# Selective scan of a 12-block decoder: two states in one scan instruction, the residual added by TensorE, the normalisation done by ScalarE

## The reference, cut to what matters

```
gate = sigmoid(x @ W_gate.T + b_gate)
x_proj, delta_proj = split(x @ W_in.T + b_in)
delta = relu(delta_proj)
A = -exp(A_log);  c0 = C_mat[0]
for each time step t:                  # h: batch x 512 channels x 16 states
    h = h * exp(A * delta_t) + (x_t * delta_t) * B_mat
    y_t = h @ c0
block = gate * (y + x_proj * D_vec) @ W_out.T + b_out
x = layernorm(x + block)
```

## Time and profile before

| | |
|---|---|
| median of 3 runs | 3064.9 us (3063.79 to 3069.06) |
| profiled execution | 3043.24 us, of which the span is 3041.4 us |
| granted TensorE clock, mean of the span | 0.972 |
| PE busy | 2806.5 us, 92% |
| DVE busy | 1905.0 us, 63% |
| ACT busy | 1218.6 us, 40% |
| POOL busy | 324.8 us, 11% |
| the scan block | from 2365 to 2705 us of the span |

### The profile page before, as it was taken

How to read it: one execution, slowest core, us unless ns; L and a number is a source line. 1 busy time by engine, 2 the same in 40 slices (tenths; PEclk the granted TensorE clock), 3 DMA queues, 4 the chain that set the end, 5 groups by cost and what they waited for, 6 DMA issues and landing times. The chain is left out here.

```text
span 3041.4 us, 52348 instructions
## 1 busy us (share of the span) xinstructions
PE 2806.5 (92%) x20888; PEld 1815.5 (60%) x20888; DVE 1905.0 (63%) x3430; ACT 1218.6 (40%) x2591; POOL 324.8 (11%) x459
## 2 busy tenths in 40 slices
PE   6999899999998979899999989899898899989898
PEld 3565456666666858566666667656565333346576
DVE  4675367777764347477777753345557999966522
ACT  1333254445542335355544431133242866633111
POOL 1111100000002700000000000000111000001232
PEclk9999999999999979899999999999999999999899
DMA  3001000000012331100000000100000000000241
GB/s 117 20 14 69 23 33 5 5 5 5 5 67 78 92 127 37 42 5 5 8 6 5 36 18 1 33 17 21 19 21 32 18 1 1 1 18 18 101 168 66
DMA packets 43246, 103.58 MB, mean 34 GB/s; under 512 B 4929, under 2 KB 32687, under 8 KB 39425
## 3 DMA queue, kind: packets, MB, share of 16 engines
q1 hardware_dynamic: 37217, 86.66, 8.1%
q0 software_dynamic: 5792, 13.59, 1.5%
HBM read 66.74 MB, written 19.07 MB: 28 GB/s over the span
## 5 line engine op out<-in xcount | busy, mean ns | idle before, releaser
L2350 ACT ACTIVATE prob<-R,neg_max 128x333 f32<-128x333 f32 x512 | 268.7, 538 | 184.0 <-DVE neg_max L2417 183.8
L3898 DVE TENSOR_TENSOR_SCAN arena<-arena,u 128x512 f32<-128x512 f32 x256 | 289.5, 1200 | 0.3 <-issue 0.2
L2238 PEld LDWEIGHTS T<-const,prob 128*128 128x128 f32 (+1 forms) x1536 | 183.6, 143 | 82.4 <-DVE prob L2430 37.0
L2430 DVE TENSOR_TENSOR prob<-prob,rec 128x666 f32<-128x666 f32 x256 | 218.4, 853 | 19.8 <-issue 0.9
L2417 DVE TENSOR_REDUCE neg_max<-R 128x2 f32<-128x666 f32 x256 | 205.8, 845 | 34.9 <-PE R L2227 34.8
L2238 PE MATMUL T<-const,prob 128*128 128x128 f32 (+1 forms) x1536 | 211.0, 274 | 13.0 <-DVE prob L2430 10.7
L2357 ACT ACTIVATE prob_t<-T 128x384 f32<-128x384 f32 x256 | 125.8, 491 | 228.4 <-PE T L2238 222.3
L3829 ACT ACTIVATE arena<-delta,neg_a 128x510 f32<-128x510 f32 x256 | 174.5, 714 | 40.2 <-DVE arena L3898 39.1
L2423 DVE COPY prob_t<-T 128x384 f32<-128x384 f32 x256 | 142.3, 556 | 39.5 <-PE T L2238 13.0
L2157 PE MATMUL O<-keys_in,arena 128*128 128x333 f32 x512 | 164.8, 444 | 0.0
L3732 PE MATMUL R<-arena,diag 64*64 64x512 f32 x1024 | 136.0, 620 | 27.4 <-DVE arena L3898 27.3
(11 more groups left out here) (590 smaller groups left out, 5341.6 us busy)
## 6 DMA issues: line engine op xcount, KB each, us to landing
w<-w_dram SPq DMA_DIRECT2D x16, 1024.0 KB, 6.9
arena<-pack_dram SPq DMA_DIRECT2D x2, 4100.0 KB, 14.6
q_pad<-q_pad SPq DMA_DIRECT2D x24, 224.0 KB, 2.7
arena<-pack_dram SPq DMA_DIRECT2D x4, 1284.0 KB, 6.6
arena<-pack_dram SPq DMA_DIRECT2D x1, 4896.0 KB, 15.3
slots_in<-x_nat SPq DMA_DIRECT2D x2, 2048.0 KB, 8.7
arena<-planes SPq DMA_DIRECT2D x8, 512.0 KB, 8.5
arena<-k_nat SPq DMA_DIRECT2D x16, 224.0 KB, 2.7
```

The source lines that it names most:

```text
L2238: last = nc.tensor.transpose(S.T[0:n, i, kc * P:(kc + 1) * P], prob[:, g % 2, i, first:first + n], S.ident)
L2350: last = nc.scalar.activation(prob[:, g % 2, i, :], S.R[:, g % 2, i * BANK:i * BANK + XK], ACT.Exp, bias=neg_max[:, g % 2, i:i + 1], accum ...
L2430: nc.vector.tensor_tensor(prob[:, g % 2, :, :], prob[:, g % 2, :, :], rec[:, g % 2, :].unsqueeze(2).to_broadcast([P, 2, XK]), ALU.mult)\
L3898: nc.vector.tensor_tensor_scan(state[:, q % HELD, :], decay[:, q % DEEP, :], u[:, i % 2, :], 0.0, ALU.mult, ALU.add)\
```

## The change

Six edits, all in `selective_scan`:

1. A scan instruction covers two states: 1024 elements instead of 512, from two adjacent ring slots. There are 128 instead of 256. The rings keep their sizes (6 and 10 slots). The scan waits for both decays. Since `u` must then stand twice in a row, ScalarE copies it (`doubled`), once a unit.
2. The first two decays and the first copy of `u` are issued ahead of the wait for `setup_bc`.
3. The residual is added by TensorE: a matmul of the identity with `x_nat` behind each bias matmul, 16 matmuls in all (32 as recorded).
4. VectorE's `residual` and `normalised` go. What stays is `spread`: statistics read straight from PSUM. It stands behind the scans of states 10 and 11, and of 12 and 13, of a leaving unit (before: behind states 12 and 15, and the two normalisations behind state 15 and behind state 2 of the next unit). The statistics have a slot for each of two batches.
5. GpSimd makes a shift, -mean * rstd, besides rstd: four instructions with two drains instead of two with one. ScalarE normalises from PSUM with scale and bias (`normalised`), at `n == 13` and `n == 15` of a leaving unit.
6. ScalarE's copy of the second batch to `x_t` moves from `n == 12` to `n == 8` of the following unit. TensorE's transposes stay where they were.

The core of the diff (left out: names of marks and buffers, `settle` calls):

```diff
                         for tt in range(TT):
                             nc.tensor.matmul(S.O[:, s, tt * D:(tt + 1) * D], part(S.const, CONST, "ones")[0:1, :],
                                              part(W, TB, "bo")[0:1, :], start=(tt == 0), stop=False, skip_group_check=True)
+                            nc.tensor.matmul(S.O[:, s, tt * D:(tt + 1) * D], S.ident, S.x_nat[:, (PAIR * g + s) * TT + tt, :],
+                                             start=False, stop=False, skip_group_check=True)
...
+            def doubled(i):
+                act.wait_ge(M.u_done, i + 1)
+                nc.scalar.activation(u[:, i % 2, 1, :], u[:, i % 2, 0, :], ACT.Copy).then_inc(M.u_twice, 1)
+
...
+            def normalised(b):
+                act.wait_ge(M.rstd_ready, b + 1)
+                for tt in range(TT):
+                    last = nc.scalar.activation(S.x_nat[:, b * TT + tt, :], S.O[:, b % PAIR, tt * D:(tt + 1) * D], ACT.Identity,
+                                                bias=shift[:, b % PAIR, tt:tt + 1], scale=rstd[:, b % PAIR, tt:tt + 1])
+                last.then_inc(M.yn_ready, 1)
...
             act.drain()
+            decays(0, 0)
+            decays(0, 1)
+            doubled(0)
             act.wait_ge(M.setup_bc, 1)
             for i in range(UNITS):
                 g, ct = i // CT, i % CT
                 for n in range(NS):
-                    decays(i, n)
+                    if i >= 1 or n >= 2:
+                        decays(i, n)
                     if i == 0 and n == 4:
                         gates(0)
+                    if i + 1 < UNITS and n == 15:
+                        doubled(i + 1)
                     if i + 1 < CT:
                         diagonal(i + 1, n)
...
-                    if n == 12 and g >= 1 and ct == 1:
+                    if g >= 1 and ct == 0:
+                        if n == 13:
+                            normalised(PAIR * g - 2)
+                        if n == 15:
+                            normalised(PAIR * g - 1)
+                    if n == 8 and g >= 1 and ct == 1:
                         transposed(PAIR * g - 1)
...
-            transposed(B - 2)
-            transposed(B - 1)
+            for b in (B - 2, B - 1):
+                normalised(b)
+            for b in (B - 2, B - 1):
+                transposed(b)
...
-                nc.vector.tensor_tensor(u[:, i % 2, :], xp[:, i % 2, :], delta[:, i % 2, :], ALU.mult)
+                nc.vector.tensor_tensor(u[:, i % 2, 0, :], xp[:, i % 2, :], delta[:, i % 2, :], ALU.mult).then_inc(M.u_done, 1)
             def scanned(i, n):
                 q = i * NS + n
-                dve.wait_ge(M.exp_done, q + 1)
+                two, held = q % DEEP, q % HELD
+                dve.wait_ge(M.exp_done, q + 2)
                 if q >= HELD:
-                    dve.wait_ge(M.state_used, q - HELD + 1)
-                nc.vector.tensor_tensor_scan(state[:, q % HELD, :], decay[:, q % DEEP, :], u[:, i % 2, :], 0.0, ALU.mult, ALU.add)\
-                    .then_inc(M.state_done, 1)
+                    dve.wait_ge(M.state_used, q - HELD + 2)
+                nc.vector.tensor_tensor_scan(state[:, held:held + 2, :].rearrange("p s n -> p (s n)"),
+                                             decay[:, two:two + 2, :].rearrange("p s n -> p (s n)"),
+                                             u[:, i % 2, :, :].rearrange("p s n -> p (s n)"), 0.0, ALU.mult, ALU.add)\
+                    .then_inc(M.state_done, 2)
...
-            def residual(b):
+            def spread(b):
                 dve.wait_ge(M.y_full, b + 1)
-                nc.vector.tensor_tensor(ysb[:, b % 2, :, :], S.O[:, b % PAIR, :].rearrange("p (t d) -> p t d", t=TT),
-                                        S.x_nat[:, b * TT:(b + 1) * TT, :], ALU.add)
-                dve.drain()
                 for tt in range(TT):
-                    nc.vector.bn_stats(S.bst[:, tt, :], ysb[:, b % 2, tt, :])
-                dve.drain()
+                    nc.vector.bn_stats(bst[:, b % PAIR, tt, :], S.O[:, b % PAIR, tt * D:(tt + 1) * D])
+                dve.drain()
+                if b >= PAIR:
+                    dve.wait_ge(M.yn_ready, b - PAIR + 1)
                 for tt in range(TT):
-                    last = nc.vector.bn_aggr(S.mv[:, tt, :], S.bst[:, tt, :])
+                    last = nc.vector.bn_aggr(mv[:, b % PAIR, tt, :], bst[:, b % PAIR, tt, :])
                 last.then_inc(M.ln_stat, 1)
...
             weighted(0)
-            dve.drain()
             for i in range(UNITS):
                 g, ct = i // CT, i % CT
+                dve.wait_ge(M.u_twice, i + 1)
                 leaving = g >= 1 and ct == 0
-                for n in range(NS):
+                for n in range(0, NS, 2):
                     scanned(i, n)
-                    if n == 7 and i >= 1:
+                    if n == 6 and i >= 1:
                         product(i - 1)
-                    if n == 9 and i + 1 < UNITS:
+                    if n == 8 and i + 1 < UNITS:
                         weighted(i + 1)
+                    if n == 10 and leaving:
+                        spread(PAIR * g - 2)
                     if n == 12 and leaving:
-                        residual(PAIR * g - 2)
-                    if n == 15 and leaving:
-                        normalised(PAIR * g - 2)
-                        residual(PAIR * g - 1)
-                    if n == 2 and g >= 1 and ct == 1:
-                        normalised(PAIR * g - 1)
+                        spread(PAIR * g - 1)
             product(UNITS - 1)
             for b in (B - 2, B - 1):
-                residual(b)
-                normalised(b)
+                spread(b)
...
                 pool.wait_ge(M.ln_stat, b + 1)
-                nc.gpsimd.tensor_scalar(S.rstd[:], S.mv[:, :, 1], EPS, None, ALU.add)
+                at = b % PAIR
+                nc.gpsimd.tensor_scalar(rstd[:, at, :], mv[:, at, :, 1], EPS, None, ALU.add)
+                nc.gpsimd.tensor_scalar(shift[:, at, :], mv[:, at, :, 0], -1.0, None, ALU.mult)
                 pool.drain()
-                nc.gpsimd.tensor_tensor(S.rstd[:], S.rstd[:], part(S.const, CONST, "neg_half")[:, 0:TT], ALU.pow)\
-                    .then_inc(M.rstd_ready, 1)
+                nc.gpsimd.tensor_tensor(rstd[:, at, :], rstd[:, at, :], part(S.const, CONST, "neg_half")[:, 0:TT], ALU.pow)
+                pool.drain()
+                nc.gpsimd.tensor_tensor(shift[:, at, :], shift[:, at, :], rstd[:, at, :], ALU.mult).then_inc(M.rstd_ready, 1)```

How the change moves instructions, as they stand in program order. First ScalarE before, around the first leaving unit (i = 4) and the unit behind it; `arena<-delta,neg_a` is a decay, `delta`, `xp`, `gated` are the next unit's projections, `x_t<-O` is a batch's copy to `x_t`:

```order
L3823 ACTIVATE gated<-T,half_bg 128x512 [waits a_qa_full]
L3829 ACTIVATE arena<-delta,neg_a 128x2x255 [waits a_state_done] x8
L3840 ACTIVATE odd<-R 128x512 [waits a_odd_full]
L3844 ACTIVATE x_t<-O 128x2x256 [waits a_yt_full]
L3829 ACTIVATE arena<-delta,neg_a 128x2x255 [waits a_state_done] x3
L3815 ACTIVATE delta<-T,arena 128x512 [waits a_qa_full]
L3829 ACTIVATE arena<-delta,neg_a 128x2x255 [waits a_state_done] x2
L3819 ACTIVATE xp<-T,arena 128x512 [waits a_qd_full]
L3829 ACTIVATE arena<-delta,neg_a 128x2x255 [waits a_state_done]
L3844 ACTIVATE x_t<-O 128x2x256 [waits a_yt_full]
```

More of the change, by code:

```diff
@@ L3661, in selective_scan @@
         xp = sb("xp", [P, 2, BANK])
-        u = sb("u", [P, 2, BANK])
+        u = sb("u", [P, 2, 2, BANK])
         gated = sb("gated", [P, 3, BANK])
@@ L3671, in selective_scan @@
         halves = sb("halves", [P, HB])
-        ysb = sb("ysb_own", [P, 2, TT, D])
+        bst = sb("bst_own", [P, 2, TT, 6])
+        mv = sb("mv_own", [P, 2, TT, 2])
+        rstd = sb("rstd_own", [P, 2, TT])
+        shift = sb("shift_own", [P, 2, TT])
         scan = part(W, TB, "scan", CT)
@@ L3877, in _ @@
             odd_part(UNITS - 1)
-            transposed(B - 2)
-            transposed(B - 1)
+            for b in (B - 2, B - 1):
+                normalised(b)
+            for b in (B - 2, B - 1):
+                transposed(b)
+            settle(act, M.u_done, UNITS)
             settle(act, M.setup_bc, 1)
@@ L3884, in _ @@
             settle(act, M.yt_full, B)
+            settle(act, M.rstd_ready, B)
         @block.vector
@@ L3969, in _ @@
                 pool.wait_ge(M.ln_stat, b + 1)
-                nc.gpsimd.tensor_scalar(S.rstd[:], S.mv[:, :, 1], EPS, None, ALU.add)
+                at = b % PAIR
+                nc.gpsimd.tensor_scalar(rstd[:, at, :], mv[:, at, :, 1], EPS, None, ALU.add)
+                nc.gpsimd.tensor_scalar(shift[:, at, :], mv[:, at, :, 0], -1.0, None, ALU.mult)
                 pool.drain()
-                nc.gpsimd.tensor_tensor(S.rstd[:], S.rstd[:], part(S.const, CONST, "neg_half")[:, 0:TT], ALU.pow)\
-                    .then_inc(M.rstd_ready, 1)
```

(3 more changed lines are left out.)

11 lines of the change are left out of this document (2 added, 9 removed).

## The result

The changed kernel takes 3093.9 us (median of 4 runs, 3091.45 to 3098.75) against 3064.59 us (4 runs), a ratio of 1.0092 with a 95% interval of 1.0069 to 1.0114. It is 29 us slower. The forecast was 3078 us with a range from 3061 to 3088: the sign was right, the size not.

What follows compares the result with a forecast made beforehand. VectorE was taken to set the pace. Three groups at +4.5 (+13.5), first group +0.5 and tail -0.9 gave +13 us on the profiled 3043.2, 3056, plus 21.7 to the runs' median: 3078 us, range 3061 to 3088.

Steps and rivals of the forecast that it cites:

- VectorE bounds the block; four decays lie ready at most: Scan block: VectorE works 323.7 of 336 us; with six decay slots, longer ScalarE hold-ups stop the scans.
- The double scan: VectorE's scans: 2.184 us a pair from start to start, saving 0.40 us a unit, 6.4 us in all.
- The leaving unit: Unit ct = 0, three of them: 25.6 us against 23.15, VectorE standing 3.5 us before states 14 and 15.
- The unit behind it: Unit ct = 1: 23.1 us against 19.04 + 0.63, VectorE standing 4.3 us for decay 9 behind the x_t copy.
- "1.92 us a group" for the identity: TensorE's added identity matmuls: four in each group at 0.48 us each, priced by the output's 1.92 for four.
- The first group, +0.5: Group without leaving batches: first scan 0.55 later, four units save 1.6, product waits 1.6; together +0.5 us.
- Low clock kept as before: TensorE in the unit behind a leaving one: the spell at 1.2 GHz kept in the sum, 1.7 us a group.
- More low clock: Rival: a second low-clock spell in each group costs up to 1.7 us each; +18, 3083 us; no chance given.
- The tail, -0.9: Behind the last scan: ScalarE's last copy comes some 0.9 us sooner.
- TensorE has 36 us to spare: Over the 336 us block TensorE is busy 299.9 us, so some 36 us are spare.
- forecast +13.5: Three groups with leaving batches: 86.5 us each against 82.0, +4.5, three times.

Runs made afterwards that it cites:

- a5_single: The changed kernel with scans of one state (512 elements) again, all else as changed; block 338.0 us.
- a6_warm: The changed kernel plus spare TensorE matmuls in each leaving unit, one ahead of summing states 12 and 13, five ahead of 14 and 15; block 337.7 us, ratio 1.0058.
- a8_grouped: The changed kernel with each group's four bias matmuls first, then its four identity matmuls, instead of in turn; block 335.9 us, ratio 1.0056.
- after_again: The changed kernel profiled a second time, nothing altered; block 345.6 us.
- b1_ident: The kernel before plus the 16 identity matmuls behind the bias matmuls, nothing else; block 329.2 us, ratio 1.0014.
- a4_both: The changed kernel with ScalarE's normalisations at n == 15 and n == 3 of the next unit, second x_t copy at n == 12; block 337.3 us, ratio 1.0034.
- a10_all: The changed kernel with biases and identities grouped, spare matmuls in the leaving unit and the second x_t copy behind decay 12; block 329.8 us.

## Why the prediction was wrong in size

- *VectorE bounds the block; four decays lie ready at most.* Right: each stop of ScalarE reached the scans. (The block's slices of the page before are 32 to 35, and ScalarE stands there at 8, 6, 6 and 6 tenths, not at 5.)
- *The double scan.* Right. 2.184 from start to start was forecast; 15.38 us for seven gives 2.185. The saving is 0.05 us a scan. The 151 cycles (by estimate 0.157 us) that the section "The TRN2 errata — SBUF-src ops pay a fixed extra latency per instruction" of the Trainium skill's page "VectorE: DVE Perf Modes" gives for a tensor_tensor lie near the fixed part of a scan's duration, 2 x 1.200 - 2.272 = 0.13 us. The section also says that many small tiles pay this latency each; back to back only 0.05 us of it shows here, and the measurement decides.
- *The leaving unit.* 25.6 us forecast, 25.8 measured. GpSimd's first instruction waited for the longer scan: 2.13 us, and 1.03 in `a5_single`. The exclusive lock of the section "SBUF: two separate sides" in the Trainium skill's page "SBUF — State Buffer" fits: 2491.56 + 2.13 = 2493.69 is the end of the scan behind the first statistics.
- *The unit behind it.* 23.1 forecast, 23.3 measured in the first of the three groups (unit starts from the product and scan rows above), 24.0 and 24.3 in the others. The place of the wait was right, its 4.3 us (3.92 measured) partly luck. TensorE began its first `summed` at 2504.88 - 2500.86 = 4.0 and not 2.4, because the low clock (to 2504.0) fell on the last summing of the leaving unit, the transposes and the skip matmul ahead of it; from there to the end of the transposes it took 8.4 and not 10.05, because the clock was full again. The two errors cancel: the transposes end at 12.4, as forecast.
- *"1.92 us a group" for the identity.* This step failed, in two ways. I took 0.48 us from four output matmuls in a row, and the new ones stand in turn with one-row matmuls. The eight take 4.9 us instead of 3.8, so the identity costs 3.0 us a group. And the sum had no term for a low clock at this place: the second spell added 3.2 us (from the first bias to what follows the output 9.98 us, against 6.74 in `a6_warm` at the full clock, 2513.54 to 2520.28). The third unit took 23.1 us instead of 19.2, twice, and 19.9 in the last group, without that spell. `a8_grouped` had neither the turns nor a spell, with no matmul left out.
- *The first group, +0.5.* It was +2.4 to its last unit's end, in part by the same step (waits of 0.67 and 2.73 where 1.6 was forecast; here the clock was low from 2415 to 2419 us as well, and `after_again`, without that, has 2.49), and the first scan began 1.15 later, not 0.55: u is copied behind two decays, and the scan waited 1.23 us.
- *Low clock kept as before.* Too low. "More low clock" was a rival at 3083 and held the right kind of loss, but I had priced it, at up to 1.7 us each, for the idle time in the leaving unit. The first spell lasted 7 and twice 10 us instead of 3, and in the last two groups the product of the unit behind waited 0.99 and 1.28. The prediction's reading that TensorE had waited most of the time for 9 us ahead of the low clock was wrong: from 2462.0 to 2471.7 us it was busy for 5.1 us.
- *The tail, -0.9.* 13.3 us from the last scan to the next block against 14.5: -1.2.
- *TensorE has 36 us to spare.* True as a mean, and misleading. In the group's second unit it is never idle from 2515.15 to 2530.87 us, and the work was added exactly there.

Sum of the block by its own terms: forecast +13.5 without start and tail, measured +27.7. Of the 14.2 between them 7.8 are two third units, 2.4 the first group, some 1.8 the last group's second and third units; about 2 are spread over the waits behind longer spells. Some 6.5 of the 7.8 are the two second spells, which are chance in part, so the term without a price is larger than the one with a wrong price.

Open: what starts the second spell. It stayed away in the profiles of `b1_ident` and `a8_grouped`, but neither the turns nor ScalarE's waits are needed for it. `a4_both`, with shorter waits, had it in all three groups. `a4_both` and `a6_warm` had it in the first group too (2431 to 2434 us), where no batches leave and nothing is normalised, and `a10_all` had it once with the pairs in order. In `after_again` only one group did.

## What to carry to other kernels

Price an added matmul by its neighbours, not only by its shape: a series of one kind is no price for two kinds in turn, and grouping them cost nothing here. Count the low clock as a term of its own wherever TensorE is the late one. Look at the slack of the one unit where work is added, not at the engine's mean over the block. Work moved to an engine that is idle a third of the time still stops the engine it feeds, if it stands in order behind a wait that lasts longer than the buffer between them.

## What the runs showed of the hardware

- A one-row (1x256) and a 128-row (128x256) fp32 matmul in turn into the same bank: 0.627 us each; in series 0.48 and 0.46 (`b1_ident`, `a8_grouped`).
- TensorE's clock fell to 0.50 not only after idle time but within 15.7 us of unbroken work (low from 2521 to 2528 us of the changed kernel), some 17 us after the spell in the leaving unit had ended.
- GpSimd's 128x2 tensor_scalar took 0.22 us beside no scan, 1.03 us beside scans of 512 elements and 2.13 us beside scans of 1024.
